# Metaformer block on one core: statistics in groups 0, 1-2, 3-4, 5-7, second layer written in side-by-side pairs, group 5 added on VectorE, last store in halves, new instruction orders

## What is computed

```python
def _ln_c(v, eps=1e-06):
    m = jnp.mean(v, axis=1, keepdims=True)
    s = jnp.var(v, axis=1, keepdims=True)
    return (v - m) / jnp.sqrt(s + eps)

# _L0_conv_ref(x) = x * (V / (V + 1e-06)), V: number of walks that visit the pixel.
# The walks' steps depend on the mean over the channels of x, which is zero up to
# rounding after _ln_c; V is then a fixed map.
x = x + _L0_conv_ref(_ln_c(x))
t = _to_tokens(x)                       # 32768 pixels of 24 channels
t = t + _L0_ffn_ref(_ln_t(t), W1, b1, W2, b2)
x = _from_tokens(t, x)

def _qlinear(x, W, b):                  # q_mul: 5 exponent, 2 mantissa bits; q_acc: 5 and 10
    y = q_acc(jnp.einsum('bsk,nk->bsn', q_mul(x), q_mul(W)))
    return q_acc(y + q_mul(b))
h = jax.nn.relu(_qlinear(x, W1, b1))    # 24 -> 96
y = _qlinear(h, W2, b2)                 # 96 -> 24
```

## Time and profile before

| | us |
|---|---|
| median of 3 runs | 71.01 (70.59 to 73.23) |
| the profiled execution | 71.21 |
| its span, first to last instruction | 69.4 |

### The profile page before, as it was taken

The page is one execution under the profiler, slowest core; times in us unless marked ns, Lnnn a source line. Parts: engine busy times, 40 slices in busy tenths (PEclk is TensorE's granted clock), DMA queues, the critical chain, the costliest instruction groups (busy, mean ns, idle before and its releaser), DMA issues.

```text
span 69.4 us, 1372 instructions
## 1 busy us (share of the span) xinstructions
PE 53.4 (77%) x486; PEld 37.7 (54%) x486; DVE 54.9 (79%) x120; ACT 44.2 (64%) x60; POOL 24.1 (35%) x25
## 2 busy tenths in 40 slices
PE   2993999999999999948859969899898989700000
PEld 1323999999999999817126427355532644600000
DVE  2059934989799999999999999999999999981000
ACT  0802241161789999238999999999999998510000
POOL 1000000009885004034199989846640326000000
PEclk9999999999999999999999999999999999995555
DMA  0899995000094900653903999989999979963940
GB/s 0 291 403 404 413 402 232 9 0 0 0 184 71 198 0 0 130 101 57 170 9 73 216 218 282 209 189 200 302 218 202 296 214 331 240 241 125 395 177 11
DMA packets 4619, 12.51 MB, mean 180 GB/s; under 512 B 512, under 2 KB 640, under 8 KB 4608
## 3 DMA queue, kind: packets, MB, share of 16 engines
q0 software_dynamic: 2016, 5.51, 39.6%
q1 hardware_dynamic: 2160, 5.90, 22.2%
q10 hardware_dynamic: 432, 0.97, 3.6%
HBM read 3.72 MB, written 3.15 MB: 99 GB/s over the span
## 4 chain that ended last, share of the span: by engine, by line
PE 28%; DVE 23%; issue 15%; ACT 15%; DMA 7%; SPq 1%; DVEq 0%; ACTq 0%
ACT hidden_rounded L426 10%; PE ps_ffn L546 8%; DMA pixels<-in_x 7%; PE ps_ffn L534 6%; PE ps_ffn L564 4%; PE ps_hidden L564 4%; DVE hidden_q L852 3%; PE ps_ffn L619 3%; DVE hidden_act L843 3%; DVE result L812 3%; ACT packed_t L417 2%; DVE packed L831 2%; ACT ffn_rounded L436 2%; DVE inv_std L788 2%; DVE inv_std L817 2%
## 5 line engine op out<-in xcount | busy, mean ns | idle before, releaser
L426 ACT ACTIVATE hidden_rounded<-ps_hidden 128x1024 f16<-128x1024 f32 x24 | 23.9, 1049 | 0.5 <-PE ps_hidden L597 0.5
L343 POOL TENSOR_TENSOR result<-centred,gain 128x768 f32<-128x768 f32 x5 | 9.4, 1887 | 17.3 <-DVE scaled_var L805 14.7
L597 PE MATMUL ps_hidden<-packed_t,w1q 96*128 96x512 fp8e5 x48 | 13.9, 380 | 1.7 <-ACT packed_t L417 1.2
L331 POOL DMA_DIRECT2D result<-pixels x8 | 9.1, 1131 | 9.1 <-DVE result L812 7.9
L843 DVE TENSOR_SCALAR hidden_act<-hidden_rounded,b1q 128x1024 f16<-128x1024 f16 x24 | 11.6, 487 | 0.1
L395 ACT ACTIVATE squares<-centred 128x768 f32<-128x768 f32 (+1 forms) x9 | 6.7, 764 | 5.2 <-DVE centred L774 5.2
L619 PEld LDWEIGHTS ps_ffn<-w2q,hidden_q 128*128 128x128 fp8e5 x168 | 7.5, 98 | 3.7 <-DVE hidden_q L852 2.0
L619 PE MATMUL ps_ffn<-w2q,hidden_q 128*128 128x96 fp8e5 x168 | 8.3, 206 | 1.3 <-DVE square_sums L781 1.2
L337 POOL DMA_DIRECT2D result<-ffn_out x6 | 6.5, 1082 | 7.6 <-DVE ffn_out L860 7.6
L564 PEld LDWEIGHTS ps_ffn<-squares,fixed 128*128 128x128 f32 x72 | 8.7, 191 | 0.6
L564 PE MATMUL ps_ffn<-squares,fixed 128*128 128x128 f32 x72 | 8.9, 276 | 0.0
(11 more groups left out here) (54 smaller groups left out, 53.8 us busy)
## 6 DMA issues: line engine op xcount, KB each, us to landing
pixels<-in_x SPq DMA_DIRECT2D x8, 384.0 KB, 6.5
result<-pixels POOLq DMA_DIRECT2D x8, 384.0 KB, 4.6
out<-result SPq DMA_DIRECT2D x7, 384.0 KB, 4.3
result<-ffn_out POOLq DMA_DIRECT2D x6, 384.0 KB, 5.4
fixed<-in_fixed ACTq DMA_DIRECT2D x1, 497.5 KB, 5.5
out<-result ACTq DMA_DIRECT2D x1, 384.0 KB, 3.2
fixed<-in_fixed ACTq DMA_DIRECT2D x1, 64.0 KB, 3.3
```

The source lines that it names most:

```text
L331: pool.dma_start(result[:, n], pixels[:, n], accum_op=ALU.add).then_inc(s.residual[n], 16)
L343: nc.gpsimd.tensor_tensor(result[:, n], centred[:, n], group_values(gain, n), ALU.mult).then_inc(s.conv_pool, 1)
L426: nc.scalar.activation(hidden_rounded[:, i % HIDDEN_BUFS], ps_hidden[:, i % 2], ACT.Copy).then_inc(s.hidden_rounded, 1)
L597: last = nc.tensor.matmul(ps_hidden[:, i % 2, b * BANK:(b + 1) * BANK], w1q[:, t * P:(t + 1) * P], packed_t[:, n % 2].bitcast(E5M2)[:, b:: ...
```

## The change

- `UNIT_SIZE` becomes [1, 2, 2, 3]: units 0, 1-2, 3-4, 5-7. The share is held for both halves of the picture, 64 KB more constants. `SUM_SETS` stays.
- `second_layer` writes through `ffn_pairs`: the 96 columns of a matmul lie at a step of two, those of b = 0 and b = 1 side by side. `round_ffn` then reads and writes runs of 384.
- `ADD_BY_DMA` is groups 0 to 4, `ADD_ON_VECTOR` 5 to 7. Group 7 is added in two halves of channels (`channel_parts`), each after both of its `second_bias`.
- SP stores groups 0 to 6 and the first half of 7; ACT the second half (`store_last`).
- New orders on PE, ACT, DVE and POOL.

```diff
-UNIT_SIZE = [1, 1, 2, 4]
+UNIT_SIZE = [1, 2, 2, 3]
 UNITS = len(UNIT_SIZE)
 ...
-FIXED = {"ident": P, "share": PIX, "w1": Q * HIDDEN, "w2": TILES * CQ, "b1": TILES, "b2": 2 * CQ}
+FIXED = {"ident": P, "share": HALVES * PIX, "w1": Q * HIDDEN, "w2": TILES * CQ, "b1": TILES, "b2": 2 * CQ}
 FIXED_AT = {name: sum(list(FIXED.values())[:i]) for i, name in enumerate(FIXED)}
 ...
-ADD_BY_DMA = range(0, 6)
-ADD_ON_VECTOR = range(6, NG)
+ADD_BY_DMA = range(0, 5)
+ADD_ON_VECTOR = range(5, NG)
 ...
         ps_late_channels = ps_ffn[:, 0, 0:4 * GPIX]
-        ps_square = [partial_sums(ps_hidden[:, 0], 1), partial_sums(ps_hidden[:, 1], 1)]
+        ps_square = [partial_sums(ps_hidden[:, 0], 1), partial_sums(ps_hidden[:, 1], UNIT_SIZE[1])]
         ps_square += [partial_sums(ps_ffn[:, 1], count) for count in UNIT_SIZE[2:]]
 ...
             return ps_ffn[:] if n < NG - 1 else ps_hidden[:, 0].rearrange("p (h m) -> p h m", h=2)
+        def ffn_pairs(n, half):
+            return ffn_banks(n)[:, half, 0:JP * CQ].rearrange("p (j m b) -> p j m b", j=JP // 2, b=2)
 ...
-        def wait_result(eng, s, n):
+        def wait_result(eng, s, n, part):
 ...
             else:
-                eng.wait_ge(s.result_vector, ADD_ON_VECTOR.index(n) + len(pixel_halves(n)))
+                eng.wait_ge(s.result_vector, ADD_ON_VECTOR.index(n) + part + 1)
+        def channel_parts(n):
+            return [(0, CH), (CH, C)] if n == NG - 1 else [(0, C)]
 ...
         def _(sp):
-            def store(s, n):
-                wait_result(sp, s, n)
-                sp.dma_start(out[n], result[:, n]).then_inc(s.stored, 16)
+            def store(s, n, part=0):
+                lo, hi = channel_parts(n)[part]
+                wait_result(sp, s, n, part)
+                sp.dma_start(out[n][:, lo:hi], result[:, n, lo:hi]).then_inc(s.stored, 16)
+            def first_groups(s):
+                store(s, 0)
+                store(s, 1)
+                store(s, 2)
+                store(s, 3)
+                store(s, 4)
+                store(s, 5)
+                store(s, 6)
+                store(s, 7, 0)
 ...
                 sp.dma_start(pixels[:, n], x[n]).then_inc(pixels_in[n], 16)
-            for n in range(NG - 1):
-                store(flat_pass, n)
+            first_groups(flat_pass)
             uneven_map = is_uneven(sp)
-            sp.wait_ge(flat_pass.stored, 16 * NG)
+            sp.wait_ge(flat_pass.stored, 16 * (NG + 1))
 ...
             def first_groups(s):
-                pool.wait_ge(s.scaled_var, 2)
+                pool.wait_ge(s.norm2, 2)
                 conv(s, 0)
+                pool.wait_ge(sums_taken, 3)
+                conv(s, 1)
                 add_pixels(s, 0)
-                pool.wait_ge(s.norm2, 2)
-                conv(s, 1)
                 add_pixels(s, 1)
                 add_pixels(s, 3)
-                pool.wait_ge(s.ffn_out, 1)
+                pool.wait_ge(s.hidden_q, 3)
                 conv(s, 4)
+                add_pixels(s, 4)
                 add_ffn_by_dma(s, 0)
-                add_pixels(s, 4)
-                pool.wait_ge(s.hidden_act, 8)
+                pool.wait_ge(s.norm2, 4)
                 conv(s, 5)
 ...
                 add_ffn_by_dma(s, 2)
-                add_pixels(s, 7)
                 add_ffn_by_dma(s, 3)
                 add_ffn_by_dma(s, 4)
-                add_ffn_by_dma(s, 5)
+                add_pixels(s, 7)
 ...
                 act.wait_ge(s.second_layer, n + 1 + part)
-                nc.scalar.activation(ffn_rounded[:, n % 2].rearrange("p (h j) m b -> p h b (j m)", h=2)[:, lo:hi],
-                                     ffn_banks(n)[:, lo:hi, 0:JP * CQ].rearrange("p h (b m) -> p h b m", b=2),
+                nc.scalar.activation(ffn_rounded[:, n % 2].rearrange("p (h j) m b -> p h (j m b)", h=2)[:, lo:hi],
+                                     ffn_banks(n)[:, lo:hi, 0:JP * CQ],
                                      ACT.Copy).then_inc(s.ffn_rounded, 1)
+            def store_last(s):
+                wait_result(act, s, NG - 1, 1)
+                act.dma_start(out[NG - 1][:, CH:C], result[:, NG - 1, CH:C]).then_inc(s.stored, 16)
 ...
             def first_groups(s):
                 square(1)
+                square(2)
                 first_std(0)
+                square(3)
                 second_std(s, 0)
                 first_std(1)
-                square(2)
                 second_std(s, 1)
                 copy_turned(s, 0)
-                square(3)
                 round_hidden(s, 0, 0)
+                copy_turned(s, 1)
                 square(4)
+                round_hidden(s, 0, 1)
                 square(5)
-                round_hidden(s, 0, 1)
                 first_std(2)
-                copy_turned(s, 1)
                 round_hidden(s, 0, 2)
 ...
                 round_hidden(s, 1, 0)
+                copy_turned(s, 2)
                 round_hidden(s, 1, 1)
-                copy_turned(s, 2)
+                round_hidden(s, 1, 2)
                 first_std(3)
-                round_hidden(s, 1, 2)
+                round_hidden(s, 2, 0)
                 round_ffn(s, 0)
-                round_hidden(s, 2, 0)
+                copy_turned(s, 3)
+                round_hidden(s, 2, 1)
                 second_std(s, 3)
-                round_hidden(s, 2, 1)
-                copy_turned(s, 3)
                 round_hidden(s, 2, 2)
 ...
                 round_ffn(s, 7, 1)
+                store_last(s)
 ...
-            wait_result(act, flat_pass, NG - 1)
-            act.dma_start(out[NG - 1], result[:, NG - 1]).then_inc(flat_pass.stored, 16)
 ...
                     for t in range(TILES):
-                        last = nc.tensor.matmul(ffn_banks(n)[:, half, at * CQ:(at + 1) * CQ],
+                        last = nc.tensor.matmul(ffn_pairs(n, half)[:, j, :, b],
                                                 hidden_q[:, n % 2, t, col * P:(col + 1) * P].bitcast(E5M2)[:, 0::2],
 ...
             def first_groups(s):
                 sum_channels(2)
+                sum_channels(3)
                 sum_squares(0)
-                sum_channels(3)
                 sum_squares(1)
+                sum_squares(2)
                 sum_late_channels(0)
 ...
                 first_layer(s, 0, 0)
-                sum_squares(2)
+                turn(s, 1)
+                sum_squares(3)
                 pe.wait_ge(var_taken, 2)
                 first_layer(s, 0, 1)
-                sum_squares(3)
+                sum_squares(4)
                 first_layer(s, 0, 2)
-                turn(s, 1)
-                sum_squares(4)
+                turn(s, 2)
                 first_layer(s, 1, 0)
 ...
                 sum_squares(7)
-                turn(s, 2)
                 first_layer(s, 1, 2)
+                first_layer(s, 2, 0)
                 pe.wait_ge(second_weights, 1)
 ...
                 second_layer(s, 0)
-                first_layer(s, 2, 0)
+                turn(s, 3)
                 first_layer(s, 2, 1)
+                first_layer(s, 2, 2)
                 keep_busy(s, 1)
-                first_layer(s, 2, 2)
-                turn(s, 3)
                 first_layer(s, 3, 0)
 ...
                 first_layer(s, 7, 2)
+                keep_busy(s, 7)
                 keep_busy(s, 6)
                 second_layer(s, 6)
+                second_layer(s, 7, 0)
                 find_peak()
-                keep_busy(s, 7)
-                second_layer(s, 7, 0)
                 second_layer(s, 7, 1)
 ...
                     dve.wait_ge(inv_std_ready, u + 1)
-                    share_u = flat_share[:, UNIT_START[u] % GROUPS * GPIX:][:, 0:UNIT_SIZE[u] * GPIX]
+                    share_u = flat_share[:, UNIT_START[u] * GPIX:][:, 0:UNIT_SIZE[u] * GPIX]
                 else:
 ...
-                lo, hi = [at * GPIX // 2 for at in pixel_halves(n)[part]]
+                lo, hi = channel_parts(n)[part]
                 dve.wait_ge(s.residual[n], 16)
-                dve.wait_ge(s.ffn_out, n + 1 + part)
-                total = result[:, n, :, lo:hi]
-                nc.vector.tensor_tensor(total, total, ffn_out[:, n, :, lo:hi], ALU.add).then_inc(s.result_vector, 1)
+                dve.wait_ge(s.ffn_out, n + len(pixel_halves(n)))
+                total = result[:, n, lo:hi, :]
+                nc.vector.tensor_tensor(total, total, ffn_out[:, n, lo:hi, :], ALU.add).then_inc(s.result_vector, 1)
 ...
             def first_groups(s):
 ...
                 centre(1)
+                take_sums(2)
+                centre(2)
                 take_var(0)
+                centre(3)
                 inverse_std(0)
-                take_sums(2)
                 conv_gain(s, 0)
-                centre(2)
                 take_var(1)
 ...
                 second_inverse(s, 1)
-                centre(3)
+                conv(s, 2)
                 second_norm(s, 1)
 ...
                 centre(4)
+                quantise(s, 2)
                 centre(5)
 ...
```

(110 more changed lines are left out.)

12 lines of the change are left out of this document (6 added, 6 removed).

## The result

The changed kernel takes 74.34 us (median; before 72.12 in the same comparison), a ratio of 1.049 with a 95% interval of 1.042 to 1.057. All ratios in this document compare only the undisturbed executions of both kernels (here 74.20 to 74.35 us against 70.59 and 71.01), because both kernels also have slower ones, up to 73.52 us before and 107.99 after. The forecast was 68.0, range 66.8 to 70.5. Its profiled execution took 74.33 us with a span of 72.5, so 1.8 us lie around the span as before.

The account below looks back on a forecast made before the run. DVE bounds the middle, transfers follow: DVE ends at 62.9, the last half issued at 62.95 lands 3.1 us later, ending 0.4, span 66.4; with 1.8 around it 68.2, less 0.2 to the median: 68.0 us, range 66.8 to 70.5.

Parts of the forecast that it names:

- Matmuls at a step: PE's 192 second-layer matmuls, writing every second column, keep their 0.043 us each; PE has room.
- the lower bound: Price of a second-layer matmul writing at a step of two: 0.043 us, as now; the forecast took this.
- the upper bound: Price of a second-layer matmul at a step: 0.084 us, double, from the fp32 matmul's 0.112 us for 128 columns.
- Rival 1: PE becomes the bound at double pitch, 0.084 us per second-layer matmul: span 68.6, 70.2 us; chance 0.18.
- Rival 2: Second-layer matmuls slow PE further, passing +2% at a pitch of 0.102 us; 75.8 us at three times 0.043; chance 0.12.
- flag behind the last add: DVE's tail: flag's 0.38 us moves last, ending near 63.3, covered by stores landing two us later.
- Landing of the last half: Final store: the last half, issued at 62.95, lands after 3.1 us (bounds 2.7 and 5.1).
- ACT's saving: Second-layer rounding: contiguous copies save 1.6 us of ACT (bounds 0 and 1.8), costed at nothing because DVE is the bound.
- Head: New statistics units: delay and moved work about even at the start; 0.2 us gained overall (0.3 lost to 1.5 gained).
- the wider constants: Loads at the start: 64 KB more, 0.1 us taken (bounds 0 and 0.16).
- Group 5 on DVE: DVE's tail: one more addition charged 0.9 us in full; removes the transfer landing at 63.48 that held store 5.
- Pixels of group 7: POOL's last add_pixels: pixels are in by 60, before add(7) wants them at 61.9.

Follow-up runs that it names:

- b_pairs: The kernel before with only the second layer's pairs side by side (step-of-two writes, ACT rounding in a row): 74.53 us, ratio 1.056.
- b_steps: The kernel before with keep_busy's matmuls replaced by six at varied write steps: bf16 0.51 us in a row, 0.83 at steps 2 to 4; fp32 1.60 at steps 1 and 2.
- a_contig: The changed kernel with the second layer writing its 96 columns in a row again and ACT interleaving as it rounds: 70.88 us, ratio 1.007.
- a_flag: The changed kernel with flag right behind the last quantise_hidden and find_peak ahead of the last second layer: 74.56 us, ratio 1.058.
- a_cf_act_run: a_contig_flag with ACT reading and writing in a row, interleaving left out, so values land on wrong pixels: times spread from 68.81 to 71.55 us.
- a_contig_flag: The changed kernel with both edits, second-layer writes in a row and flag early: 70.56 us, ratio 0.999.
- a_one_pass: a_contig_flag without the second pass (handling of an uneven map, not run with these inputs) on any engine: 68.96 us, ratio 0.975.
- b_flag_last: The kernel before with flag moved behind the last add and nothing else: 71.59 us, ratio 1.013.
- a_cf_act_reads: a_contig_flag with ACT reading PSUM's two blocks alternately and writing in a row, not reading in a row and writing at a step: 69.56 us, ratio 0.988.
- b_add5: The kernel before with group 5 added by DVE right behind flag, not by a transfer: 69.78 us, ratio 0.987.

## Why the prediction was wrong, step by step

- *Matmuls at a step: the step that failed.* The forecast took the lower bound, 0.043 us, "what these matmuls cost now is the pace of 96 columns going through, which the step leaves alone". It measured 0.081, and PE, not DVE, then set the pace. That the upper bound of 0.084 came so close is luck: 0.112 us is one of the two records of an fp32 matmul (the 12 "matmuls" of a group are six, in 12 records), and by the matmul the same row would have given 0.168. The page of the Trainium skill cited against the change, "PSUM — Partial Sum Buffer", Specifications (TRN2), is borne out for these matmuls: b_pairs, 4.1 us on the last add. Its "any" is too wide for fp32 operands, where b_steps shows no loss. Against a rule that spoke of just this stood one assumption that no row showed; rivals 1 and 2 together deserved more than 0.30. It cost the forecast 3.8 us by the table (47.03 against a_contig's 43.23), and 4.7 with ACT's copy equally fast (a_flag's 47.83 against a_cf_act_run's 43.08, which differ in the matmul's target alone).
- *Rival 1* had the right pitch and the wrong price, 2.2 us for 4.1. It let PE hide 0.68 us a group. From the second layer of group 1 to that of group 6, b_pairs took 60.01 - 37.67 = 22.34 us against 19.53, 0.56 us a group of the 0.92 added: PE works in order, and only 0.36 of its gaps stood where they helped. Rival 2 put "slower" at a pitch of 0.102; it came at 0.081.
- *flag behind the last add, costed at nothing because "the stores land two us later".* Wrong by 2.6 us of the ending. It counted flag's 0.38 us, not what every engine does after it: PE's end came 4.4 us behind it, and the stores covered only 1.6 us of that. This is not the net price of the place: with the flag early the landings grow, and neither a_flag (74.56 against 74.34) nor a_contig_flag (70.56 against 70.88) shows a gain clear of the noise. What is shown to cost time is the second pass itself, by a_one_pass. In the kernel before, the flag's late place costs 0.8 us (b_flag_last).
- *Landing of the last half.* 3.1 us was taken; 1.9 to 2.0 measured where the flag is late or the second pass gone, 2.9 to 3.7 where engines jump while stores drain. The estimate from the Trainium skill, "DMA: Bandwidth & Descriptors", Anatomy of one DMA, 2.45 us, lies between. In the forecast's own condition, a flag at the end, it is 1.2 us in the change's favour: 4.6 - 1.2 + 2.6 = 6.0 of the 6.1 us by which the span was missed.
- *ACT's saving, "cost at nothing".* Nearly right for the old order, where it moved the last add by 0.24 us (43.87 and 43.63 in the table) though DVE was 98% busy. Wrong for the new one, where it is worth 0.89 (43.99 and 43.10): there DVE idles 1.58 us in a_contig's middle (37.04 busy from 20.68 to 59.30) where before has 0.86, and 1.00 in a_cf_act_reads.
- *Head.* Even, as worked out: sums of 4-7 reach DVE at 20.49 (forecast 20.27), variance of 5-7 at 31.88 (31.6), PE waits 1.31 (1.5). The 0.2 us gained did not show: from PE's first channel sum to the last add the new units and orders are 0.1 us behind the old ones with ACT's short copy (57.05 and 56.93) and 0.8 with the long one (58.00 and 57.16; a_contig's middle is busy 37.32 of 39.03). For the wider constants 0.1 us was taken; PE's first channel sum starts at 6.01 to 6.64 in six traces without them and at 6.30 to 7.67 in ten with them, so their price stays open and may be more.
- *Group 5 on DVE.* Right, in kind and in price: 0.987 alone, and 0.89 us on the last add (44.76 against 43.87), as taken; the other 0.36 of b_add5's 1.25 stood in the head.
- *Pixels of group 7.* Right: add(7) never waited.

## What to carry to other kernels

A layout that saves one engine a stride hands it to another: let the engine that reads at a step for free take it, here ACT, and measure the writer before the bound is moved onto it. Whatever comes last is followed by every engine's own end: behind the flag that took 4.4 us here. An early flag moved this end under the stores and slowed them in turn; only leaving the untaken pass out helped. Two traces can differ by 1 us before the edited part starts, so count an effect from a point that the edit can't reach. Slack of an in-order engine is worth only what stands ahead of someone's wait; here about half.

## What the runs showed of the hardware

- A matmul written to PSUM at a step of 2, 3 or 4 fp32 places takes 0.84 ns a column instead of 0.45 (0.081 and 0.043 us for 96); with fp32 operands, 0.87 ns a column and record anyway, the step is free.
- ACT's copy of 768 fp32 columns to float16 takes 829 or 860 ns reading PSUM at a step and 810 to 866 reading in a row, 1068 writing at a step of two.
- A second pass that isn't run costs 1.6 us at the end (span 68.5 against 66.9), and packets of the instruction queues stand among the last stores, one of them near 1 us long.
